# Writing the gathers' table in 33 blocks of 128 positions a batch instead of 48 units of 88

## What is computed

```python
x = x + L0(_gn(x))      # 1x1 projections, 3x3 neighbourhood attention + dynamic 3x3 kernel, projection
x = x + _modulated_dcn(_gn(x), w_off, b_off, w)

def _modulated_dcn(x, w_off, b_off, w):
    om = conv3x3(x, w_off) + b_off                 # 27 channels: 9 taps x (dy, dx), 9 masks
    py, px = base_y + ky + off_y, base_x + kx + off_x   # per position and tap
    y0, x0 = floor(py), floor(px); ly, lx = py - y0, px - x0
    v = samp(y0, x0)     * (1-ly)*(1-lx) + samp(y0, x0+1)   * (1-ly)*lx \
      + samp(y0+1, x0)   * ly*(1-lx)     + samp(y0+1, x0+1) * ly*lx      # 256 channels each
    v = v * sigmoid(mask)
    return einsum('bckhw,ock->bohw', v, w)         # 9 taps, 256 -> 256 channels
```

## Time and profile before

| | us |
|---|---|
| median of three runs | 5400.81 |
| the profiled execution's own time | 5390.38 |
| its span, first to last instruction | 5388.6 |
| mean granted TensorE clock in it | 0.972 |

### The profile page before, as it was taken

One profiled execution on the slowest core, in us unless ns is written; L12 is line 12 of the kernel. 1 busy time (PEld: TensorE's weight loads), 2 busy tenths in 40 slices (PEclk: granted clock), 3 DMA queues, 4 the chain that ended last, 5 costly groups with the idle time before them and its releaser, 6 DMA issues. The chain is left out here.

```text
span 5388.6 us, 80437 instructions
## 1 busy us (share of the span) xinstructions
PE 4889.6 (91%) x26816; PEld 2678.9 (50%) x26816; DVE 4392.5 (82%) x11212; ACT 2297.6 (43%) x5430; POOL 2282.9 (42%) x2311
## 2 busy tenths in 40 slices
PE   7868999999989998999989999899998989988888
PEld 4435554555545555455544555445554555544443
DVE  5656888878887888878888788888888878898998
ACT  2234444344443443534445344343444444443554
POOL 0003444444453444434444444444444344454776
PEclk9979999999999999999999999999999999999999
DMA  4326778877798777977779777887778877788999
GB/s 162 122 93 208 271 248 291 304 250 264 247 318 285 251 266 245 337 269 259 257 251 338 250 258 256 277 315 250 275 254 292 297 252 263 251 305 308 387 398 353
DMA packets 493125, 1451.51 MB, mean 269 GB/s; under 512 B 47396, under 2 KB 117420, under 8 KB 492460
## 3 DMA queue, kind: packets, MB, share of 16 engines
q0 software_dynamic: 331776, 1208.11, 64.3%
q1 hardware_dynamic: 160940, 238.27, 12.6%
HBM read 1309.60 MB, written 136.59 MB: 268 GB/s over the span
## 5 line engine op out<-in xcount | busy, mean ns | idle before, releaser
L730 POOL DMA_INDIRECT G<-table,IDX x2304 | 2282.0, 990 | 3066.6 <-DVE V L1381 2269.6
L749 PE MATMUL ps<-VT,s_wconv 128*128 128x512 f32 x4608 | 2277.5, 618 | 39.7 <-DVE R L1165 39.7
L1381 DVE SCALAR_TENSOR_TENSOR V<-G,WT,V 128x256 f32<-128x256 f32 x4608 | 2019.1, 479 | 122.6 <-DVE V L1381 3.2
L1109 ACT ACTIVATE VT<-ps 128x512 f32<-128x512 f32 x1152 | 686.0, 595 | 2390.0 <-PE ps L955 2387.9
L749 PEld LDWEIGHTS ps<-VT,s_wconv 128*128 128x128 f32 x4608 | 828.7, 194 | 871.7 <-issue 836.1
L1374 DVE SCALAR_TENSOR_TENSOR V<-G,WT 128x256 f32<-128x256 f32 x2304 | 1006.5, 477 | 84.0 <-ACT G L1098 40.1
L1129 DVE TENSOR_TENSOR E<-ps,s_band 128x512 f32<-128x512 f32 x1024 | 649.5, 682 | 455.3 <-PE ps L811 273.3
L955 PEld LDWEIGHTS ps<-s_ident,V 128*128 128x128 f32 x4608 | 574.5, 143 | 755.8 <-issue 754.5
L1098 ACT ACTIVATE G<-G,WT 128x256 f32<-128x256 f32 x1850 | 841.2, 499 | 111.0 <-DMA G<-table,IDX 110.1
L955 PE MATMUL ps<-s_ident,V 128*128 128x128 f32 x4608 | 708.8, 277 | 86.4 <-DVE V L1381 84.4
L787 PE MATMUL ps<-XN,s_wqk 128*128 128x512 f32 x1024 | 490.1, 606 | 14.8 <-ACT XN L1011 14.6
(11 more groups left out here) (101 smaller groups left out, 2764.9 us busy)
## 6 DMA issues: line engine op xcount, KB each, us to landing
table<-E SPq DMA_DIRECT2D x384, 176.0 KB
G<-table,IDX POOLq DMA_INDIRECT x2304
X<-in_x SPq DMA_DIRECT2D x64, 512.0 KB, 7.3
x<-X SPq DMA_DIRECT2D x64, 512.0 KB, 7.0
R<-x SPq DMA_DIRECT2D x64, 512.0 KB
out<-R SPq DMA_DIRECT2D x64, 512.0 KB, 5.8
G<-in_x SPq DMA_DIRECT2D x56, 512.0 KB, 4.4
s_wconv<-in_wconv SPq DMA_DIRECT2D x1, 2304.0 KB, 9.2
```

The source lines that it names most:

```text
L730: e.indirect_dma_start(G[a % NG][:, :], None, T[b % 2], bass.IndirectOffsetOnAxis(ap=IDX[b % 2][:, col:col + 1], axis=0)).then_inc(d_g[a % ...
L749: mm = e.matmul(CV[oh][:, :], s_wconv[:, h, t, oh * P:(oh + 1) * P], VT[U % 2][:, h, :], start=(t == 0 and h == 0), stop=(t == 8 and h == 1))
L1109: e.activation(VT[U % 2][:, :, 2 * P * pair:2 * P * (pair + 1)], BK[banks.place[use]][:, :].rearrange("p (h n) -> p h n", h=2), ACT.Copy). ...
L1381: e.scalar_tensor_tensor(vt[:, :], gt[:, q * C:(q + 1) * C], wt[:, col, q:q + 1], vt[:, :], ALU.mult, ALU.add).then_inc(lerp[q - 1], 1)
```

## The change

The border rows are part of the flat order of the padded image, so the table can be cut anywhere. 64 rows of 66 positions are 4224 = 33 x 128. The change cuts each batch into 33 blocks of 128 positions; a block belongs to the first chunk whose rows (with the halo row below) cover it, and `table_blocks(c)` lists the blocks of chunk c in pairs: chunks 0, 1, 2 and 4 to 7 have 4 blocks (two pairs), chunk 3 has 5 (two pairs and a single).

```diff
+def table_blocks(c):
+
+    last = lambda n: min((RO * (n + 1) + 1) * EW, H * EW) // P
+    lo, hi = last(c - 1) if c > 0 else 0, last(c)
+    return [list(range(k, min(k + 2, hi))) for k in range(lo, hi, 2)]
...
         elif kind == "tp":
-            for i in range(3):
+            for i in range(len(table_blocks(s[2]))):
                 banks.take(("tp", g, i))
         elif kind == "om":
             if s[3] == 0:
-                for i in range(3):
+                for i in range(len(table_blocks(s[2]))):
                     banks.give(("tp", g, i))
-                for n in range(2):
-                    prods.take(("tt", g, n))
+                    if i % 2 == 0:
+                        prods.take(("tt", g, i // 2))
                 banks.take(("om", g))
...
-                    for i in range(3):
+                    for i, blocks in enumerate(table_blocks(c)):
                         e.wait_ge(*freed(("tp", g, i)))
                         k = prods.place["tt", g, i // 2]
                         for half in range(2):
-                            pos = (RO * c + 1 - half) * EW + 176 * i
-                            dst = T[b % 2][pos:pos + 176, half * C:(half + 1) * C].rearrange("(a p) c -> p a c", p=88)
+                            pos = (1 - half) * EW + P * blocks[0]
+                            dst = T[b % 2][pos:pos + P * len(blocks), half * C:(half + 1) * C].rearrange("(a p) c -> p a c", p=P)
...
-                        for a in range(2):
+                        for a, block in enumerate(blocks):
                             for h in range(2):
-                                pos = EW + 88 * (2 * i + a)
-                                mm = e.transpose(BK[banks.place[use]][0:88, (2 * a + h) * P:(2 * a + h + 1) * P],
-                                                 flat[:, h, pos:pos + 88], s_ident[:, :])
+
+                                pos = P * block - (RO * c - 1) * EW
+                                mm = e.transpose(BK[banks.place[use]][:, (2 * a + h) * P:(2 * a + h + 1) * P],
+                                                 flat[:, h, pos:pos + P], s_ident[:, :])
...
-                        e.activation(rows_of(g, i), BK[banks.place[use]][0:88, :], ACT.Copy).then_inc(freed(use)[0], 1)
+                        e.activation(rows_of(g, i), BK[banks.place[use]][:, 0:C * len(blocks)], ACT.Copy).then_inc(freed(use)[0], 1)
```

More of the change, by code:

```diff
@@ L340, in rotations @@
             banks.give(("om", g))
-            for n in range(2):
+            for n in range((len(table_blocks(s[2])) + 1) // 2):
                 prods.give(("tt", g, n))
@@ L600, in need_rows @@
         def need_rows(e, k, g):
-            n = sum(2 - key[2] for key, v in prods.place.items() if v == k and key[0] == "tt" and key[1] <= g)
+            n = sum(len(table_blocks(key[1] % NCH)[2 * key[2]:2 * key[2] + 2])
+                    for key, v in prods.place.items() if v == k and key[0] == "tt" and key[1] <= g)
             if n > 0:
@@ L606, in rows_of @@
         def rows_of(g, i):
-            return E[prods.place["tt", g, i // 2]][0:88, CH * (i % 2):CH * (i % 2 + 1)]
+            n = len(table_blocks(g % NCH)[i])
+            return E[prods.place["tt", g, i // 2]][:, CH * (i % 2):CH * (i % 2) + C * n]
         def norm_parts(j, b):
```

## The result

| | before | after |
|---|---|---|
| median of nine runs, us | 5401.79 (5399.81 to 5404.84) | 5388.01 (5381.96 to 5390.71) |
| the profiled execution's own time, us | 5390.38 | 5390.71 |
| mean granted TensorE clock in it | 0.972 | 0.967 |

The ratio of the medians is 0.9971, with a 95% interval of 0.9961 to 0.9981. So the change saves 13.8 us, 0.3% (15.7 us by the means). The prediction was 5375 with a range of 5363 to 5390: the sign was right and the time lies inside the range, but the gain is half of the forecast 26 us.

What follows compares the result with a forecast made beforehand. PE was taken to bound the offset phases: seven give 23 us, batch 0's gives 3.3, everything else 0, so about 26 us off the median 5400.8 gives 5375, with a range of 5363 to 5390.

Steps and rivals of the forecast that it cites:

- The 240 transposes at 0.109 us, 26 us: Offset phases: 30 fewer PE transposes a batch, 240 in all, at 0.109 us each, take about 26 us off.
- The weight load overlaps: PE's transposes: the longer load for 128 columns overlaps the matmul before, so nothing is taken off the gain.
- ACT's copies, the DMAs, banks and buffers at 0: Table building: fewer copies and DMAs and freer banks and buffers were each taken as 0 us of gain.
- DVE, four fifths busy, keeps up: Offset phases: DVE, busy 81%, keeps up, so a us taken off PE is a us off the time.
- Batch 0's chunk at 6.7 us: Batch 0's offset phase, running alone: a chunk should take 6.7 us in place of 7.12.
- The clock at 0: Whole kernel: the sum held no clock term; the offset phase at 1.00 stays dense and no idle piece is added.
- the prediction's own price of 40 us for 0.01: Whole kernel: 0.01 of mean clock is worth about 45 us times 0.9, the share bound by PE.
- a rival of 0.05: Slower by the clock: more pieces in layer 1 draw PE's clock down and eat the gain; chance 0.05.
- Absorbed by half: Offset phases: other late work makes PE's idle share grow; half of 26 us gives 5388; chance 0.13.
- the weight load: Rival for PE's transposes: longer loads set the pace, leaving a gain of 16.7 us, 5384; chance 0.06.
- the check of busy time: Sign to look for over the whole kernel: PE's busy time should fall by 25 to 27 us.
- a mean clock under 0.97 with PE's busy time unchanged would be the clock: Sign for the rival in which PE's granted clock falls; at 0.970 the time would be about 5415; chance 0.05.

Runs made afterwards that it cites:

- the fourth group: The change, before, and the change with idle filled at chunks 5 and 6, on one chip; the change took 5385.52 us, before 5399.61 us.
- the first group's chip: Chip running before, the change, before with fewer transposes, and the change with 96 a batch; the change took 5504.28 us, ratio 0.9952.
- the third's: Chip running before, the change, and the change with 112 filler matmuls ahead of attention's first half of heads; ratios of the last two 0.992 and 1.0032.
- the first result: The original nine-run measurement of the unaltered change against before: median 5388.01 us against 5401.79 us, ratio 0.9971.
- the second group: On one chip with before: the change, 5471.89 us; the change with 30 transposes a batch fewer, 5455.48 us; with 60 more, 5516.89 us.
- the two sites filled: The change with four overwritten matmuls ahead of the second half of heads in attention chunks 5 and 6; 5393.69 us, ratio 0.9989 to before.
- the first filler: The change with two overwritten 512-column matmuls ahead of the first half of heads in attention chunks 1 to 7; 5527.5 us, ratio 1.0032 to before.

## Why the prediction was half right

**The 240 transposes at 0.109 us, 26 us: right.** At equal clock four groups on four chips give 28.1, 22.8, 26.3 and 30.0 us, 26.8 on average; with 0.42 in place of the half 27.6, 24.7, 28.1 and 27.8, 27.1 on average. The spacing did not change with the width. Leaving out the transposes alone gives the gain (22.7), and putting them back takes it away.

**The weight load overlaps: right.** It went from 123 to 142 ns and nothing followed. The Trainium skill, page "TensorE: Matmul & The Clock Gate", section "LDWEIGHTS (loading the stationary operand)", has the load grow with its columns; an estimate from that page is 33 ns here. The trace has 19, and with as many transposes as before the kernel is not slower, so in this kernel the load is not the pace, whichever of the two numbers one takes.

**ACT's copies, the DMAs, banks and buffers at 0: right** as far as the kernel with 96 wide transposes can tell (7 us of gain to 10 us of cost). ACT's 28 us less of busy time bought nothing, as an engine at 42% suggests.

**DVE, four fifths busy, keeps up: right.** It went from 106.9 to 109.8 us in 132, and PE's share stayed at 97%.

**Batch 0's chunk at 6.7 us: right**, 6.70.

**The clock at 0: wrong, and it is the step that failed.** The prediction named the mechanism, gave it 0.05, and took as evidence against it that the offset phase has a clock of 1.00 and that "the change adds no idle piece". Both are true, but they don't bear on it. What fell is the clock in layer 1, a stretch of which not one instruction changed, behind idle pieces that were there before; 301 us at 1.2 GHz became 358 in the profiles. It had set 0.0065 of mean clock against the whole gain. In the fourth group the clock is 0.0026 lower, and the gain is 16.3 us where the sum had 26; the 10 us between them are the prediction's own price of 40 us for 0.01. Half of the time at 1.2 GHz would be 53, and PE's busy times give 45. What it lacked was not the price but a term in the sum: by these four chips a shift of the work moves the clock either way, by what half of the time at 1.2 GHz makes 14 us slower to 12 us faster. With that beside 26 us instead of in a rival of 0.05, 5375 would have stood with some 5363 to 5389.

**Absorbed by half**, at 5388, gives the measured time to the microsecond, and is still not the reason. PE's share in the offset phase is what it was, PE's idle time from 434 to 4915 us grew by 4 us (the wait for DVE's product went from 66.1 to 70.1 us, against the row above), and on three of the four chips the full 25 us and more arrive. A time that fits a rival does not show its mechanism. The range reached up to 5390 for this rival and for the weight load, and neither came; the clock, which took the 12 us, was left out of it. That the range held is luck.

**Where the check of busy time misled.** The prediction wanted PE's busy time to fall by 25 to 27 us. It fell by 2.0, which taken alone reads as if the work had not gone. The prediction had the right sign too, "a mean clock under 0.97 with PE's busy time unchanged would be the clock", and that is what came: 0.967 in the profile, 0.9688 in the nine runs. Busy time is in us and contains the clock; the number that tells the work is the count of instructions, or busy time in stretches at a clock of 1.00.

**Open.** Why the change draws the clock down on the chip of the fourth group, leaves it on one and raises it by 0.002 on two others; it decides between a gain of 14 and of 37 us. The profiles at least agree with the clocks: at the wait ahead of `pv` there are 5 falls before and 14 after where the clock fell, but 22 and 21 on the first group's chip and 12 and 9 on the third's, one profile each. The clocks of before's runs in the first result aren't on record but for the profiled one, so that the clock took the missing 12 us there too rests on that profile and on the fourth group. And the price of a transpose in the second group, 0.082 in place of 0.109, where a part of the work doesn't show in the time.

## What to carry to other kernels

Price a transpose, or any short matmul, by the spacing within a run, not by the mean duration, and check on a shape from the same kernel whether wider weights change it; work taken off a PE that is 97% busy came back nearly whole at equal clock here, 23 to 30 us of 26. Then put the clock into the range with its own spread, a quarter of a per cent here, when PE waits anywhere in the kernel, even in stretches that the change doesn't touch. And before a small difference is explained, take the clock out of it: compare the mean clocks first, run on more than one chip, and read the waits only then.

## What the runs showed of the hardware

- On the chips of the first result and the fourth group, between 434 and 4915 us, every fall of the granted clock, 47 in before, 60 in after and 45 with the two sites filled, begins in or within 2 us behind an idle of PE of 1.2 to 2.6 us, but most such idles (144, 155 and 141 of over 1 us) draw none, and the same length can do either: two idles of 2.34 and 2.55 us, 43 us apart, stood ahead of 1.97 and of 3.52 us for the same work, and 2.64 us in before ahead of 1.97.
- One program on one core had a mean clock of 0.961, 0.963, 0.964 and 0.972 on four chips, and takes 5531, 5509, 5505 and 5400 us. Between the ends the time at 1.2 GHz differs by 136 us, which at 0.42 to 0.5 explains 57 to 68 us of the 131; the rest is something else.
- In the profiles of before and of the change on the chips of the first result and of the fourth group the periods of the batches come in two values, 645.2 to 645.7 and 648.2 to 648.8 us, and nothing between. On the other chips they spread from 651 to 669 us. A gain of 2.7 us in a batch doesn't show in its period; it shows only where a period falls into the other value, or at the ends. I have no run that explains it. With the idles filled four of the six lie between, at 646.8 to 648.1 us.
- A float32 matmul with 512 moving columns is two instructions of 0.43 us each in the trace, which made the first filler twice as long as intended.
